# Both gates of the scan layer's front computed by ScalarE's own SiLU function, in place of a hyperbolic tangent and a product on VectorE

## The reference, cut to what matters

```python
def _silu(x):
    return jax.nn.silu(x)                     # x * sigmoid(x)

def _L0_attn_ref(x, ln_g, ln_b, W_in, conv_w, conv_b, W_xp, W_dt, b_dt, A_log, D, W_out):
    xn = layernorm(x) * ln_g + ln_b
    xh, z = jnp.split(xn @ W_in, 2, axis=-1)  # 512 channels each
    conv = causal convolution of xh with 4 taps, plus conv_b
    xc = jax.nn.silu(conv)                    # first gate
    xpj = xc @ W_xp                           # B (16), C (16) and one column for dt
    dt = jax.nn.softplus(xpj[..., -1:] @ W_dt + b_dt)
    dA = jnp.exp(dt[..., None] * A)           # 16 states per channel
    dBx = dt[..., None] * Bm[:, :, None, :] * xc[..., None]
    h = dA * h + dBx ; y = sum over states of h * C   (along the 256 positions)
    y = y + xc * D
    out = y * jax.nn.silu(z) @ W_out          # second gate
    return out + residual
```

## Time and profile before

| | before |
|---|---|
| median of three runs | 1348.92 us (1346.61 to 1349.28) |
| the profiled execution's own time | 1343.34 us |
| its span, first to last instruction | 1340.8 us |
| PE busy | 1188.1 us (89%) |
| DVE busy | 1040.3 us (78%) |
| ACT busy | 799.6 us (60%) |
| POOL busy | 201.4 us (15%) |
| mean granted TensorE clock | 0.97 |

### The profile page before, as it was taken

The page is one execution under the profiler, slowest core; times in us unless marked ns, Lnnn a source line. Parts: engine busy times, 40 slices in busy tenths (PEclk is TensorE's granted clock), DMA queues, the critical chain, the costliest instruction groups (busy, mean ns, idle before and its releaser), DMA issues.

```text
span 1340.8 us, 16987 instructions
## 1 busy us (share of the span) xinstructions
PE 1188.1 (89%) x6026; PEld 948.7 (71%) x6026; DVE 1040.3 (78%) x1644; ACT 799.6 (60%) x1994; POOL 201.4 (15%) x258
## 2 busy tenths in 40 slices
PE   5787668978999899989999999999999998989884
PEld 3554556666868778777878787878787787757863
DVE  4999899899889995999599887998699863243215
ACT  4433554568566865597468755776587646536624
POOL 0100110111211221221202120212121200000002
PEclk8888889999999999999999999999999999989998
DMA  6412010233403331332314240241242200000301
GB/s 241 169 44 79 23 49 23 64 63 80 111 16 80 85 75 43 82 86 36 95 24 100 63 111 8 60 103 35 93 91 64 47 24 21 0 1 9 124 0 63
DMA packets 41191, 86.67 MB, mean 65 GB/s; under 512 B 3738, under 2 KB 14971, under 8 KB 40467
## 3 DMA queue, kind: packets, MB, share of 16 engines
q1 hardware_dynamic: 27282, 60.42, 13.7%
q0 software_dynamic: 13824, 25.17, 10.9%
HBM read 54.38 MB, written 6.04 MB: 45 GB/s over the span
## 4 chain that ended last, share of the span: by engine, by line
PE 51%; DVE 26%; ACT 12%; issue 8%; POOL 1%; DMA 1%; ACTq 0%; DVEq 0%; SPq 0%; POOLq 0%
PE bank L296 15%; DVE scans L556 8%; PE bank L1176 5%; PE bank L511 4%; DVE scans L552 4%; PE bank L1221 4%; DVE scans L561 4%; PE bank L713 4%; ACT scans L532 3%; PE bank L1194 3%; PE bank L907 3%; PE bank L668 3%; PE bank L901 2%; DVE nmax L1330 2%; PE bank L1183 2%
## 5 line engine op out<-in xcount | busy, mean ns | idle before, releaser
L556 DVE TENSOR_TENSOR_SCAN scans<-scans 128x1024 f32<-128x1024 f32 x128 | 292.4, 2284 | 11.3 <-ACT scans L529 5.4
L532 ACT ACTIVATE scans<-dt,a_neg 128x255 f32<-128x255 f32 x512 | 221.4, 502 | 0.1
L511 PE MATMUL bank<-scans,ident 128*128 128x256 f32 x640 | 177.2, 411 | 28.0 <-DVE scans L561 22.7
L511 PEld LDWEIGHTS bank<-scans,ident 128*128 128x128 f32 x640 | 124.8, 204 | 64.9 <-DVE scans L561 29.5
L589 POOL DMA_DIRECT2D scans<-scans x96 | 84.6, 882 | 524.2 <-DVE scans L561 524.1
L1264 ACT ACTIVATE ya<-bank,nmax 128x256 f32<-128x256 f32 x256 | 107.0, 472 | 85.5 <-DVE nmax L1330 85.2
L561 DVE TENSOR_TENSOR scans<-scans,BC 128x1024 f32<-128x1024 f32 x128 | 155.9, 1218 | 1.7 <-ACT BC L417 0.4
L552 DVE TENSOR_TENSOR scans<-conv,BC 128x1024 f32<-128x1024 f32 x128 | 155.6, 1215 | 0.0
L1330 DVE TENSOR_REDUCE nmax<-bank 128x2 f32<-128x512 f32 x128 | 87.2, 682 | 78.7 <-PE bank L1176 78.2
L1194 PE MATMUL bank<-v,ya 128*128 128x65 f32 x1024 | 129.9, 270 | 0.7 <-ACT yo L1255 0.7
L1194 PEld LDWEIGHTS bank<-v,ya 128*128 128x128 f32 x1024 | 127.3, 193 | 2.8 <-ACT ya L1271 0.9
(11 more groups left out here) (270 smaller groups left out, 2186.0 us busy)
## 6 DMA issues: line engine op xcount, KB each, us to landing
BC<-xpj_scratch SPq DMA_DIRECT2D x31, 1024.0 KB, 5.9
scans<-scans POOLq DMA_DIRECT2D x96, 256.0 KB, 3.3
xin<-in_x SPq DMA_DIRECT2D x8, 256.0 KB, 2.8
conv<-in_x SPq DMA_DIRECT2D x8, 256.0 KB, 2.8
out<-scans SPq DMA_DIRECT2D x8, 256.0 KB, 2.1
kept_x<-x SPq DMA_DIRECT2D x7, 256.0 KB, 2.0
kept_w<-wa SPq DMA_DIRECT2D x7, 256.0 KB, 2.0
BC<-kept_w SPq DMA_DIRECT2D x1, 1792.0 KB, 8.9
```

What stands on the lines that cost most here:

```text
L511: last = pe.matmul(sums_of(c), ident[:, :], step_of(b, u)[:, i, :], start=False, stop=(h == UH - 1 and i == SUMMED[b] - 1), skip_group_che ...
L532: ins = act.activation(step[:, j, 1:S], dt[b % 2][:, c, 1:S], ACT.Exp, scale=a_neg[:, c, n:n + 1])
L556: dve.tensor_tensor_scan(flat(H[:, :, :]), flat(H[:, :, :]), flat(dBx), 0.0, ALU.mult, ALU.add).then_inc(s["a_scan"], 1)
```

## The change

Four pieces of code change. ACT's two gate instructions use `ACT.Silu` with a scale of 2 (which undoes the halving) and signal the semaphores `a_xc` and `a_silu_z`, which DVE signalled before. The 32 `scalar_tensor_tensor` instructions of DVE (L446 and L455) and their two semaphores go. And the order strings of all five engines are other ones: DVE's is 32 letters shorter, the others have the same letters in another order. ACT's strings stand below whole; those of PE, DVE, POOL and SP are left out.

```diff
...
     "act": (
-        "FFFFFFFFFSSSSSSFSSFFSSSSFFSSFSSWSSSSSSSSSSFFSSFSSFSSFFFFFSSSSSSSWFSSWFFSSFFSSWSSSFFWSSSWWSSFSSWSSWFWSSFWSSWSSW"
-        "WSSWWWWYSSSSYYSSYYSWFYWSYSYYSYYSWYYSSYYYFFYYSSWFYYYSSWYYWSYYYSYYSSYYYWYYWWYYYSSFSSYYWFSSYYYWSYYSWFYYYSSYWFSSYW"
-        "YYYWYFYFWWYSSSSYYSSYSWYYFWWSSYWYWYYSYSWFWYYFSSYYWYYYWWYFSSWSSWWYYYYSSWWFSSWYYYFWSYYSFSSYYYWYYWSYSWYYSYYWWYYWYS"
-        "SYYSWFYWSYSWYYWWYFWYYYYFWWYWYSSSSSWWYWYSSWYYYWSWYSFYYWSSWYYWWSSWYWYFFSSYYYWWSSYWYFSSWYYYFSSYYFYYYWFSYYWSYYYWSS"
-        "YYFSSWYYYWWYYSWSYYWYSSWYYWSSWYYFYWYYYYFYYWWWYYWWWSSFWSSYSSYWSYYWFFYSSWYWYWFWYYSYSWYWYSSYYYFWYYWWYYSYSYSYWSSSYY"
-        "YFSSYYFWYYYWYYWYYYFSSSWSYYWWYYYWSYYSWSFYYWYYFSWSSYWYSWSYYYWWWYYWWWYWYYYWWYSFSYYSWSSWSYYWYSFFYWYFYYWYWYYSSYYSWY"
-        "WSYYWSSYYWYYYSSSSYYYWSSYYWFYYWYYYWSSWYWYYYYSWSYYYYWSSWYWSYYWSWSSYYWSWSYYWSSFWWYWYWYYYWYWYWWYWYSYSSSYYWSSSYYWWY"
-        "YSYSWWYSYSWYSYYSWYYYFSSYYSWSWYYYFWYYSSYYYWYYWWSSYYWYYWYSSWSYSWYYYWWSSYSSYYSYYSSSWWWYYWWWWYYWYYWYWWYYSWYYWYYWYW"
-        "YYYYYWWYYYYYWYYYWYYYYYWYYYYYWYYWYYYYYWYYYWWYYWYYWYYWWYWWWYWYYYWYYWWYWYWYYYWYYWYYYYYWYYYWYYWYYYYYWYYYYYWYYYWYYY"
+        "FFFFFFFFFSFSSFSSSSSFFSSFFSSSSSSSWSSSSSSSSSSSFFSSFFSSFFFFFSSSSSSSWFSSWFFSSFFWSSFSSFWFWSSFWFSSWSSWWSSWWSSWSSWWSS"
+        "WSSSSWWYYYYYYYYSYYSYSSSSSYYWFYYYSSWYYFSSFYYYFSYYSFWYYYFFYYSSWYYWFYSYYSWYYYSSYYSSYYYWWYYFWSSWYYSSWWYYSSWYWSYSWS"
+        "SYSYYSFWWWYYWWWWYYWWYYWWWSSSSSSSWYWFWYSYYYWYWSSSWYYSYYSWFYFYYYYSSWYYYWSSFYWYYYYFSSWWYYWSYWSYYWYYWYSSWSSWYYWSSY"
+        "YYSYYSYYYSYSYSYYSYYWFWWYYFWWYYWYYWYWYWSSYSSSSYYWYWSFFYYWSSYYWYSSYYSYYYSWYYWFSSSYYYWFSYYWSSWYYYFFSSWFYYFSSYYYFY"
+        "YWFSSYYWYFSSYYFWYYYYFSSYWYYWWSYYSSSWYWWWWWWYWSSFSYYSSYYWSYSWWSYWSYWYYWYSSFFWYYSSYYYWYYWWFYWSSWWYYYYSWWSSYWYSYS"
+        "WSYYFYYYFWYYFWSSYYYSWSYYSFFWSYYYWWYYWSSWYYWYYSSWYWSYYSWYYWWFYYWWWSSWSYSSYWSYYSWYWYWYWSSFWSSYSYSYWWYYWSSSYYYFFW"
+        "WSYYSWSFYYYSSYYWFYYYFSSYYFWSYYWSYFYYWSSWYYYWWYYSSYYWSYSYWYSYYWSYYWWWYYYYYWWYWYSSSWWSWSYSWYSYYSWSWYYWSYWSYYWYYW"
+        "YWYYYWYYSSYYSWYWSYYWSSYYWYYYSSSSYYYWYYWYWYYYYSSWSWYYSWYYYWSSWWYYWYYSWSYWYYYYSSWWWSSYYWWWWYYWWYYWYWYWYWYYYWYWYY"
+        "YYWYYYYYSYYWYYWYYYWYYYYYWYYWYYYWYYYYYWYYYWWYYWYYWYYWWYWWWYWYYYYWYWWYWYWYYYWYYWYYYYYWYYYWYYWYYYYYWYYYYYWYYYWYYY"
         "YYYYWYYYYWYWYYYYYWWWWWWWWWWWWWWWWWWWW"
     ),
...
-    a_x=16, a_var=1, a_rstd=1, a_norm=T, a_xnT_ps=1, a_xnT=KD, a_in_ps=4, a_tap=4, a_conv=4, a_z_tanh=2, a_silu_z=2, a_xc_tanh=2,
+    a_x=16, a_var=1, a_rstd=1, a_norm=T, a_xnT_ps=1, a_xnT=KD, a_in_ps=4, a_tap=4, a_conv=4, a_silu_z=2, 
...
@@ -401,7 +400,7 @@
             for j in range(2):
                 act.wait_ge(*of("a_conv", b, 2 * j + 2))
                 x, y = [flat(a[:, 2 * j:2 * j + 2, :]) for a in (xc, conv[b % 2])]
-                act.activation(x, y, ACT.Tanh).then_inc(s["a_xc_tanh"], 1)
+                act.activation(x, y, ACT.Silu, scale=2.0).then_inc(s["a_xc"], 1)
                 yield
             act.wait_ge(*of("a_xpj_ps", b))
             act.activation(xpj, f0[0:2 * NS + 1, 0:S], ACT.Copy).then_inc(s["a_xpj"], 1)
@@ -418,7 +417,7 @@
                     yield
             for j in range(2):
                 act.wait_ge(*of("a_in_ps", b, j + 3))
-                act.activation(flat(zg[b % 2][:, 2 * j:2 * j + 2, :]), f0[:, :], ACT.Tanh).then_inc(s["a_z_tanh"], 1)
+                act.activation(flat(zg[b % 2][:, 2 * j:2 * j + 2, :]), f0[:, :], ACT.Silu, scale=2.0).then_inc(s["a_silu_z"], 1)
                 yield
 
         def front_dve(dve, own, b):
@@ -440,20 +439,10 @@
                     if k < TAPS - 2:
                         own.wait()
                 yield
-            for j in range(2):
-                dve.wait_ge(*of("a_xc_tanh", b, j + 1))
-                x, y = [flat(a[:, 2 * j:2 * j + 2, :]) for a in (xc, conv[b % 2])]
-                dve.scalar_tensor_tensor(x, x, 1.0, y, ALU.add, ALU.mult).then_inc(s["a_xc"], 1)
-                yield
             dve.wait_ge(*of("a_dt", b))
             dve.wait_ge(*of("a_xc", b))
             dve.tensor_tensor(flat(conv[b % 2][:, :, :]), flat(dt[b % 2][:, :, :]), flat(xc[:, :, :]), ALU.mult).then_inc(s["a_dtx"], 1)
             yield
-            for j in range(2):
-                z = flat(zg[b % 2][:, 2 * j:2 * j + 2, :])
-                dve.wait_ge(*of("a_z_tanh", b, j + 1))
-                dve.scalar_tensor_tensor(z, z, 1.0, f0[:, :], ALU.add, ALU.mult).then_inc(s["a_silu_z"], 1)
-                yield
 
         def front_pool(pool, own, b):
             pool.wait_ge(*of("a_var", b))
```

More of the change, by code:

```diff
@@ L47 @@
     "pe": (
[L48 to L56, removed]
+        "FFFFFFFFSWSWFWSFFSYYYSYYSYYSWYYSYYSYYSYYSYSFSFSSFSFFSFSSFSWWSWFSWFSWFSFFWWSWFSFWSWWSWWWSWWSWWWSWWWSWWSWYSYSYYY"
+        "YYYYYSYSSYYSYYWWYYYYYYYSWYYYFSYYYWYYSYFYYYWFYYYFFSYYYWYSYWWYYYYSYYYSYYYWYYWWYWSWYSYWYYWWSWYYWWSWYWWSWWYSYYFYYY"
+        "YSWYFWYWYSWYWYYWYYWYSWWSSWSWWWWYYWYSYYYWWYSWWYYYWYSYYFYWYYYYSYYYWYSYWWYYYYFSWYYYWWYSWWYYYWYWWYYSWSWYWYYWSYYYWY"
+        "SYYWYYYSWYYYWSYYFYYSYYYYYSWFWYYYYWYYYWYSYWSSYSYWFYWYYWYWYYYWWSYYYWSYYYWYSYYWYYYWFYSSYYFWYYYSWWYYYWSFWYYYWFYYSY"
+        "FYYYFSYYYWFSYYYWWYYYFSYYYWFYYWSYYWSYYYSYWWWSWWWWWWWWWSWSSYSYYYYYYYWYYWYSYWYWYYWSYFWYYYWYSYWYYYYWYWWWSWWWYYYYSS"
+        "YWWYWWYYSWYYYWFYYYSSFYYYFWYYYWWYYYSFYWYYWYWYWYWSYWYYWWYSWYYWWSYYSWWYWYWYYWYYSYSFWSSWYYWYWYYYYWYYWSWYWYSYWFWSYY"
+        "WSWYWYWYYWSYYYSFWWYYYWSWYYYWSYYYFYYYWFYYSYFSYYYWFYWYYWSYYYWWYYYSWWYYYWSYWYYWYSWYYYWYSWYWWWSYYWYYWYWYYSYSSWYSYW"
+        "YWYWYYWYYSYWYWYYWSYWYYWYWYWYYWYWYYWYYYSYYYSWWYWYYWSYWYYYYWSSYYYYYYWYWYWYYYYSYSWYYWWYYWWYYSWYWWYYWYSWWYYWWWYWYY"
+        "WYSYYYYWYSWSSYWYWYWYYWYYWYWYYWYSWWYWYYWYWYWYYYYYSWYYYSYYYYYYWWYWYYYYWYYYWYYYYYYWYYYWYYYYWYYYWYYYWYYYWWWYYWYYWW"
         "YYYYWWWWWWWWYYYYYYYYWYYWYYWYWYYWYYYYWYYYWYYYWYYYWYYYWYYYWYYYWYYYWYYYWYYYWYYYYYYYYYYYYWYYYWYYYYYYYYWWWWWWWWWWWW"
@@ L72 @@
     "dve": (
[L73 to L81, removed]
+        "FWWWFFFSSSSFSWSSWSWSSWSYSSYSYSSYSYSSYSYSSYSYSSYSYSSYSYSSYSYSSYSFSSWSFSSSSSSSSSFSFSSSSSSSSSFSSSFSSWSSSWSFSSFSWS"
@@ new lines @@
+        "SWSWSSSSSWSWSSSSSWSSSWSSSWSSSWSSSSSSYSYSYSYSYSSSYYSYSSSYSYSFYSSYSYFYSWSSYYSWYSSYSYFYSSWSYSYSWYSWYYSSFYSSSWSYSS"
+        "WSYWSSSYWSSSSSWSWSSWYSYSSSSYYSWYWWYSSSSWSSSSYSSWYYSFSYSSYWSSYSYWYSSYYSFYWSWWYYSSSSYSWSYSWYSSYWSYSSSWYSSYSYSYSS"
+        "SYWYSSSYSWWSSSYSSFYSFSYYYYSWWSSSYWYYSSSYSSWSYSYSSYSSYSYSSYWSSYSYSSYSSFYYSSWSFYSWYYSSYSFSSYSYFSYSWSYWYWSSYSSSSS"
+        "WSSYSSSYWSWSWWSWWSSSYYSYSSYSYSSFYYWSWSSYSWYSYSYSFYSWSSSSSWYYSSYSSYSWSYSWYYSSYSSFYFYWSYWWSYSYSSYWWSSYSSYWSSSYSW"
+        "SSSSWSYWWYSSSSYYSSSYWSYWWSYSSSSYSYSSWFSYSWSSYYSSSYSSFYYSWSYSSYSYWYSFYSYSYSWSWWYYSSSSYSWYWSYSYSSYWSSYSSSWSYSSWW"
@@ L82 @@
+        "WYSYSSSYSYSSSYWSSYWWYSSYYSSWYSSSSYSWYYYSYSYSSSYWSSYYWYYSSYSSSYWSYWYWSSYSWSYYWSSSSYWSYSSWYSSSWWWSYSYSSSYYSWYWWY"
+        "YSWYYYWYYSYSYYYYYYWYWYYYYYWWYWYYYYYWWWYYWWWWYYYYYYYWWYYYWYYYYYWYYYYYYWYYYWYYYYYYYWWWWWWWWWWWW"
     ),
     "pool": (
-        "FFFSWWFWSSSSWSSWSSSSSSSSSSFSYWWSSSSWSSSSSSWWSSSSSFSSWWYSSSWSSSSSWSWSSSSSFSSSWWYSSWSSSSSWSWSSSSFSSSSSWWYSWSSSSS"
-        "WSWSSSSSSSSWWYSSWSSSSSWSWSSSSSSSSWWSYSSWSWWYWWWWYWWWWWW"
+        "FFFSWWFWSSSSWSWSSSSFSSSSSWSWYSSWSSSSSWWSSSSSSSSSSWWSYFSSWSSSSSSSSWWSSFSSSSSYSWWSSSSWSSSSSWSWSFSSSSSSWWYSSWSSSS"
@@ L86 @@
+        "SSWSSWSSSSSSSWWYSSSWSSSSSWWSSSSSSSWWSYSWSWWYWWWWYWWWWWW"
     ),
     "sp": (
-        "WFWSFWWSWWSFFSSSSFFSSSSSSFFSSSSWWWWFSFSSSWSWWWFSFSSSWWWWFFSSSSSWWWWFSSSSSWWWWSSSWWWWWWWWW"
+        "WFFWSWWSWWSFFSSSFSFSSSSSFFSSSSWWWWSFSFSSSWSWWWSFFSSSSWWWWSFFSSSSWWWWSFSSSWSWWWSSWWWWWWWWW"
     ),
```

## The result

The changed kernel took 1391.67 us, a median over four runs (1389.38 to 1394.06); the kernel before took 1349.1 us beside it. The ratio is 1.032 with an interval of 1.029 to 1.034, so it is slower by some 43 us. I had forecast +22 us, 1371 us, in a range of 1345 to 1403.

The account below looks back on a forecast made before the run. DVE was taken to bound the first 340 us, PE the stretch from 340 to 1030 us. Terms: -0.7 - 7 - 2 + 1 + 28 + 3 = +22 us, on a 1348.9 us median 1371 us, range 1345 to 1403.

Parts of the forecast that it names:

- The mechanism: On ACT, Silu needs its own table load against Exp, Tanh and Softplus: 71 loads where 17 were.
- VectorE's relief: 32 products (21.6 us) leave DVE: gains of 0.7 us before 40 us, 7 to 340 us, 2 to 1030 us.
- The 2 us that the prediction put there: DVE relief from 340 to 1030 us: 2 us of 12.2 us gained, between 0 and 12.2, the rest mostly waiting.
- The late loads, idling: Batches 3 to 7: 19 load pairs idle PE 1.47 us each (0.57 per us of ACT), +28 us, between 0 and 49.
- The wait that the prediction named: PE may not write the next head's scores before ACT's Copy; that wait was to grow by 15 to 25 us.
- The clock: PE's granted clock falls after gaps at some of the 19 late pairs: +3 us, between 0 and 7.
- The early loads: Batches 0 to 2: 16 new loads cost +1 us, between 0 and 9.
- in the first 340 us this is the rule: In the first 340 us a load on ACT runs ahead of its instruction's wait for PE and costs nothing.
- full price: Rival: every load among the heads costs in full, 49 us plus 7 clock, 5 early; +51 us, 1400 us, chance 0.16.

Follow-up runs that it names:

- e1: Changed kernel with Tanh in Silu's place, product left out, new order kept, 17 loads instead of 71: 1340.13 us, ratio 0.994 to the kernel before.
- e2: The change (Silu, no products on VectorE) in the order of before, 72 loads: 1389.61 us, ratio 1.0296 to the kernel before.
- e3: Kernel before with only VectorE's 32 products left out, Tanh and old order kept, 17 loads: 1342.5 us, ratio 0.9952.
- e10: Kernel before with the zeros at the head of a unit (L518) written by Exp instead of Copy: 1348.03 us, ratio 0.9999.
- e4: Kernel before with Silu in Tanh's place and the products kept, 72 loads: 1394.49 us, ratio 1.034.
- e6: Changed kernel with Silu only in batches 3 to 7, Tanh without its product in batches 0 to 2, 55 loads: 1376.48 us, ratio 1.0228.
- e8: Kernel before with Relu in Softplus's place, 1 load instead of 17: 1339.15 us, ratio 0.9931.
- e9: Changed kernel with the zeros at the head of a unit (L518) written by Exp instead of Copy, 71 loads: 1385.42 us, ratio 1.0284.
- e7: Changed kernel with the first xc piece moved right before the second in batches 1 to 7, 57 loads: 1373.88 us, ratio 1.019 to the kernel before.
- e5: Changed kernel with Silu only in batches 0 to 2, Tanh without its product in batches 3 to 7, 33 loads: 1357.22 us, ratio 1.0076.
- e11: Changed kernel with both the moved xc pieces (57 loads) and the zeros written by Exp: 1367.32 us, ratio 1.0146 to the kernel before.

## Why the prediction was right in sign and short in size

**The mechanism was right.** The table loads are the cost: 71 of them were forecast by walking the order string, 71 are in the trace, and e1 takes the whole slowdown away with them. `Silu` shares no load with `Exp` or `Softplus`. Against `Tanh` the prediction was wrong: `Tanh` ran behind `Silu` without a load (e2). The count of 71 does not depend on it. The gates cost ACT what the tanh cost. The new order costs nothing that shows.

**VectorE's relief** was put at 9.7 us; it is 6.5 us in the old order (e3) and 8 us in the new (e1). As forecast, most of the 21.6 us became waiting, and what pays lies in the early stage. From batch 3's first scan to the last scan the products are worth nothing: that part takes 691.3 us before and 691.8 in e10, and 692.1 without the products (e3); with the loads it is 726.9 (e4) and 726.7 (e2). The 2 us that the prediction put there were 0.

**The late loads, idling.** 28 us were forecast. In e6 the span is 1379.3 us with PE busy for 1211.6, in e1 1338.4 with 1195.4: PE idles 168 instead of 143 us, 25 us more for 19 pairs, 1.3 us a pair. This term held, and e8 bears its rate out. The wait that the prediction named grew by 18.5 us, PE's wait for the `Copy` of a head (waited for, us in total, times, longest), first in e1, then in e6:

```profile
PE bank L1165 <- ACT ya L1260: 21.5, 21, 3.0
PE bank L1165 <- ACT ya L1260: 40.0, 33, 3.4
```

The mechanism can be seen line by line. PE, DVE and ACT of the changed kernel at the first gate of batch 3:

```profile
291.27 0.63 ACT L403 ACTIVATE xc<-conv 128x512 f32<-128x512 f32 x1
291.92 1.28 ACT L1253 ACT_TABLE_LOAD   x1
293.21 0.84 ACT L1253 ACTIVATE ya<-bank,nmax 128x256 f32<-128x256 f32 x2
293.94 0.60 ACT L1260 ACTIVATE ya<-bank 128x512 f32<-128x512 f32 x1
...
294.59 1.13 PE L1165 MATMUL bank<-kzE,qT 128*128 128x256 f32 x4 [2.56 <-ACT ya L1260]
...
295.76 0.69 DVE L1319 TENSOR_REDUCE nmax<-bank 128x2 f32<-128x512 f32 x1 [2.15 <-PE bank L1165]
```

The same pieces in e1:

```profile
276.60 0.62 ACT L403 ACTIVATE xc<-conv 128x512 f32<-128x512 f32 x1
...
277.12 0.82 ACT L1253 ACTIVATE ya<-bank,nmax 128x256 f32<-128x256 f32 x2
...
277.83 0.59 ACT L1260 ACTIVATE ya<-bank 128x512 f32<-128x512 f32 x1
...
278.61 1.03 PE L1165 MATMUL bank<-kzE,qT 128*128 128x256 f32 x4
```

Without the loads the scores of the next head follow at once; with them PE waits 2.56 us for the `Copy` of the head before, and DVE 2.15 us for PE. From the kernel before to the changed one, DVE's wait for the scores (L1319 for L1165) grew from 78.2 to 107.0 us, but PE's for that `Copy` only from 31.4 to 40.2 us, where 15 to 25 us more were forecast: the new order by itself had taken it down to the 21.5 us of e1.

**The clock was mis-sized: 3 us forecast, 11 to 16 measured.** PE executes the same 6026 matmuls in all kernels, so its busy time shows how long they took. In the four profiled executions with 17 loads and the softplus (before, e1, e3, e10) it is 1188.1, 1195.4, 1195.0 and 1202.5 us, mean 1195; in the four with 71 or 72 (the changed kernel, e2, e4, e9) 1208.9, 1217.6, 1223.6 and 1209.2, mean 1215. So matmuls take about 20 us more in all. e6, with 55 loads, has 1211.6 us, 16 more than the first four. One execution differs from another by 7 us to either side, so this is known to some 5 us. The granted clock is on record for every execution and can be set beside it: one less the clock, times the span, is 51 us in the mean of e1's four executions, 62 in e6's and 67 in the changed kernel's. By this estimate the late loads cost 11 us of clock and all 54 cost 16. Two stretches of the changed kernel around gates of batches 4 and 5 (the last but two columns are the granted clock):

```profile
443.00:457.00 14.00, 8.13 (x38) 6.46 (x37) 8.02 (x15) 9.04 (x20) 3.91 (x5) 0.76 0.28 63
609.00:625.00 16.00, 11.52 (x53) 7.76 (x52) 12.10 (x23) 12.90 (x25) 3.13 (x5) 0.79 0.33 85
```

PE idled for 4 to 6 us in each, and its clock was at the lower of its two levels (1.2 of 2.4 GHz) for part of them. My estimate halved the price on the ground that gaps after a gate are shorter than after a softplus. But the two `xc` pieces of a batch bring four loads within 8 us (batches 3 and 5) to 20 us (batch 4), so the gaps stand close together. That this nearness is the cause is argued, not shown. These two are the lowest of twelve stretches read around gates; in six of the twelve the clock was 1.00, among them one of 30 us with 5.2 us of idling. For it: with the two pieces together (e7) the mean granted clock is 0.957, against 0.952 in the changed kernel, means of four executions each.

**The early loads were mis-sized: 1 us forecast, 12 to 18 measured (e5).** In e5's trace 12 us are lost when batch 3's scan begins (398.6 us in e1, 410.3 in e5). The other 4 us of the spans come later, where e5 has no new load and PE's matmuls took 6 us longer than in e1, as can happen between two executions. The step that failed was "in the first 340 us this is the rule": that a load falls into one of ACT's waits. The earlier trace rows showed one load that did, and the earlier trace rows a stretch in which DVE stayed full. In the changed kernel's timeline of ACT only 5 of the 70 loads after the first are followed by more than 0.1 us of waiting. PE, ACT and DVE at the gates of batch 2 show where the delay goes:

```profile
164.60 1.28 ACT L403 ACT_TABLE_LOAD   x1
...
165.89 0.63 ACT L403 ACTIVATE xc<-conv 128x512 f32<-128x512 f32 x1
166.58 3.27 PE L295 MATMUL bank<-xc,w_xp 128*33 128x256 f32 x8 [4.62 <-ACT xc L403]
...
171.60 0.59 PE L295 MATMUL bank<-wa,ones 128*128 128x256 f32 x2
...
172.31 0.88 DVE L779 TENSOR_SCALAR wa<-bank,rn 128x256 f32<-128x256 f32 x2 [1.74 <-PE bank L295]
...
175.89 2.28 DVE L545 TENSOR_TENSOR_SCAN scans<-scans 128x1024 f32<-128x1024 f32 x1
...
181.40 1.28 ACT L420 ACT_TABLE_LOAD   x1
182.70 0.60 ACT L420 ACTIVATE zg<-bank 128x512 f32<-128x512 f32 x1
...
183.35 3.50 PE L295 MATMUL bank<-xnT,w_in 128*128 128x256 f32 x8 [2.44 <-ACT zg L420]
...
189.12 0.19 DVE L798 COPY low<-bank 128x32 f32<-128x32 f32 x1 [3.91 <-PE bank L295]
```

The same products of PE in e1:

```profile
158.51 2.87 PE L295 MATMUL bank<-xc,w_xp 128*33 128x256 f32 x8 [2.35 <-ACT xc L403]
...
173.20 2.00 PE L295 MATMUL bank<-xnT,w_in 128*128 128x256 f32 x8 [0.69 <-ACT zg L420]
```

The gate is late by its loads, and PE waits 4.62 us for it, where it waits 2.35 us without them. Behind that product PE has a product of the `W` stream, which is late too, and DVE has the `W` piece L779, which needs it, in its own order ahead of the next scan: DVE waits 1.74 us. At the first `z` piece the same happens once more: PE waits 2.44 us (0.69 in e1), and DVE 3.91 us for what stands behind it on PE. In e1 DVE waits at neither place. The scan that begins at 165.88 us here begins 5.8 us earlier in e1, from what went before; the next one, at 175.89 us, begins 7.6 us earlier (168.27), and the one two units later, at 196.02 us, 13.1 us earlier (182.94). So DVE was full in the first 340 us, but not independent: its order holds pieces of other streams that come from PE, and PE's fixed order stands still at a late gate. I had looked at one softplus of batch 1, around which no such piece stands, and took ACT's idle time for cover without asking what waits for each delayed instruction.

**The sum again.** In the prediction's terms: -6.5 to -8 for the products; +25 idling and +11 to +16 clock for the late loads; +12 to +18 for the early ones. That is +40 to +53, for the 43 measured. The trace divides it more sharply, by stage and without adding runs up. The columns are those of the earlier trace rows; first e1, then the changed kernel, each up to batch 3's scan and from there to the last scan:

```profile
0.00:399.00 399.00, 328.38 (x1392) 247.11 (x1393) 334.28 (x464) 211.18 (x511) 53.65 (x62) 0.90 0.26 80
399.00:1069.00 670.00, 635.30 (x3413) 520.38 (x3413) 588.68 (x883) 460.30 (x1179) 135.86 (x156) 1.00 0.31 69
...
0.00:415.00 415.00, 328.32 (x1390) 246.32 (x1391) 334.60 (x463) 241.98 (x533) 53.90 (x62) 0.90 0.26 77
415.00:1121.00 706.00, 650.19 (x3414) 526.57 (x3414) 590.14 (x882) 502.83 (x1211) 131.58 (x156) 0.98 0.29 66
```

The first stage became 16 us longer with 23 new loads, all of it idling of PE. The second became 36 us longer with 31: 21 us of idling and 15 us of longer matmuls, with the granted clock at 0.98 instead of 1.00. Behind the last scan nothing changed.

The measured time lies in the stated range, but not because the terms were right: late idling was, and the clock and the early loads were each too small by some 10 us or more. The rival "full price", at 1400 us with a chance of 0.16, was nearer in its number than the forecast, and not in its terms: it had 49 us of late idling where 25 were measured, and 5 us for the early loads. The 54 loads last 69 us, and 51 of them came through.

The Trainium skill ("ScalarE: Activation LUTs", section on what a load costs) gives 1283 ns and a drain of 1380 ns for a switch. The 71 loads here took 1283 ns each, and in the timelines above the instruction after a load that has nothing to wait for begins 1.29 or 1.30 us after the load did, with the one before ending 0.02 us ahead of it. No drain is to be seen. Its rule to group calls by table set is borne out by e7: 17 us for 14 loads.

## What to carry to other kernels

Before a function of ScalarE is exchanged for another, walk ScalarE's own instruction order and count the changes of table. Here an exchange saved 32 products on VectorE, worth 0.2 us each, and added 54 loads, worth 0.9 us each. For the price of a load, look on which instruction the engine's waits stand: a load ahead of a waiting instruction runs inside the wait, one behind it does not. And when a change gives TensorE many more short gaps, add the slower clock to the idling: here it was some 15 of 51 us.

## What the runs showed of the hardware that was not expected

- A table load waits for the semaphore of an instruction ahead of it that needs no table (L518 waits 2.98 us, the load follows at 191.17), but not for the one of the instruction that it serves (e9: the load at 180.69, its instruction at 183.65). What that is worth in time stays open: e9 and e11 are each some 4 to 6 us faster than without the edit, with intervals that meet or overlap a little.
- `Tanh` needed no load behind `Exp` and none behind `Silu`, while `Exp` and `Silu` needed one between them (e2: L1037 at 736.06).
- With the added loads the same 6026 matmuls took some 20 us longer in all (1195 to 1215 us, means of four profiled executions each). In the new order alone it is 13.5 us (e1 1195.4, changed kernel 1208.9).
- Leaving out 32 instructions of 0.68 us on an engine that is busy for 78% of the span, and for 93% of its first quarter, gave only 6.5 us, and nothing of it behind the start of batch 3's scan.
